# Mirrored score blocks in a symmetric attention, and a first stage ordered by what it needs, in a fused two-layer kernel on one core

## What is computed

```python
# layer 0, on g = groupnorm(x): attention over positions and a squeeze gate
q, k, v = Wq @ g + bq, Wk @ g + bk, Wv @ g + bv
out = v @ softmax(q.T @ k, axis=-1).T
y = sigmoid(relu(mean(g) @ se_w1.T) @ se_w2.T)
x = x + gamma * out + g * y
# layer 1, on tokens t = (batch, 2304, 128)
s = layernorm(t);  t = t + softmax(s @ s.T, axis=-1) @ s
u = layernorm(t);  t = t + top-2-of-8 experts(u)     # router softmax, gates renormalised
```

## Time and profile before

| | |
|---|---|
| time, median of 3 runs (lowest to highest) | 2839.08 us (2837.59 to 2839.95) |
| the profiled execution's own time | 2836.02 us |
| its span | 2834.2 us |
| TensorE busy | 2636.5 us, 93% |
| VectorE busy | 2161.3 us, 76% |
| ScalarE busy | 2023.1 us, 71% |
| GpSimd busy | 446.9 us, 16% |
| mean DMA rate | 8 GB/s |
| chain that ended last, by engine | PE 61%, DVE 23%, ACT 9%, issue 5%, POOL 2% |

### The profile page before, as it was taken

How to read it: one execution, slowest core, us unless ns; L and a number is a source line. 1 busy time by engine, 2 the same in 40 slices (tenths; PEclk the granted TensorE clock), 3 DMA queues, 4 the chain that set the end, 5 groups by cost and what they waited for, 6 DMA issues and landing times.

```text
span 2834.2 us, 45738 instructions
## 1 busy us (share of the span) xinstructions
PE 2636.5 (93%) x15334; PEld 2381.2 (84%) x15334; DVE 2161.3 (76%) x5499; ACT 2023.1 (71%) x4305; POOL 446.9 (16%) x840
## 2 busy tenths in 40 slices
PE   5999989999899998999989999999999999999996
PEld 4888978889788897889978898888988889888895
DVE  4886778787787877877778777887777877788775
ACT  2777767677676876768767687676867768677774
POOL 0000210032100331003200133001220022200223
PEclk7999999999999999999999999999999999999997
DMA  1000000000000000000000000000000000000000
GB/s 35 1 1 18 7 6 1 18 7 6 7 1 18 7 6 7 1 18 7 9 4 1 18 7 11 2 1 18 10 9 1 1 21 6 9 1 1 4 9 12
DMA packets 10037, 23.05 MB, mean 8 GB/s; under 512 B 1992, under 2 KB 8528, under 8 KB 8784
## 3 DMA queue, kind: packets, MB, share of 16 engines
q1 hardware_dynamic: 9808, 20.14, 2.0%
HBM read 10.70 MB, written 9.44 MB: 7 GB/s over the span
## 4 chain that ended last, share of the span: by engine, by line
PE 61%; DVE 23%; ACT 9%; issue 5%; POOL 2%; SPq 0%; DMA 0%; ACTq 0%; DVEq 0%; POOLq 0%
PE ps L1005 17%; PE ps L1007 17%; PE ps L1006 17%; PE ps L1018 9%; DVE mx L818 6%; DVE pt_lo L828 3%; DVE pt_lo L902 3%; ACT pt_hi L612 2%; ACT p_rows L600 2%; DVE u_tok L879 1%; ACT p_rows L647 1%; POOL u_rs L518 1%; ACT pt_hi L656 1%; ACT p_rows L681 1%; DVE acc L984 1%
## 5 line engine op out<-in xcount | busy, mean ns | idle before, releaser
L612 ACT ACTIVATE pt_hi<-ps 128x384 fp32r<-128x384 f32 x864 | 425.4, 492 | 319.2 <-PE ps L1018 313.5
L828 DVE TENSOR_TENSOR pt_lo<-ps,pt_hi 128x384 fp32r<-128x384 f32 x864 | 479.5, 556 | 178.7 <-ACT pt_hi L612 170.3
L600 ACT ACTIVATE p_rows<-ps,negmax 128x512 f32<-128x512 f32 (+1 forms) x720 | 464.8, 647 | 72.9 <-DVE negmax L822 65.8
L902 DVE TENSOR_TENSOR pt_lo<-p_rows,pt_hi 128x768 fp32r<-128x768 f32 x432 | 413.9, 959 | 124.1 <-ACT pt_hi L656 122.4
L818 DVE TENSOR_REDUCE mx<-ps 128x1 f32<-128x512 f32 (+1 forms) x720 | 442.0, 633 | 79.4 <-PE ps L1007 55.4
L1018 PE MATMUL ps<-ident,p_rows 128*128 128x128 f32 x2736 | 455.7, 275 | 40.4 <-DVE pt_lo L828 22.9
L647 ACT ACTIVATE p_rows<-ps,shift 128x768 f32<-128x768 f32 x432 | 389.6, 902 | 119.1 <-PE ps L1007 114.0
L1018 PEld LDWEIGHTS ps<-ident,p_rows 128*128 128x128 f32 x2736 | 332.4, 140 | 153.8 <-issue 54.9
L656 ACT ACTIVATE pt_hi<-p_rows 128x768 fp32r<-128x768 f32 x432 | 365.6, 846 | 40.1 <-PE ps L1007 0.7
L1005 PE MATMUL ps<-pt_hi,v_hi 128*128 128x384 f32 x864 | 358.6, 415 | 2.5 <-ACT y_out L621 2.5
L1005 PE MATMUL ps<-xt_hi 128*128 128x384 f32 x864 | 305.2, 353 | 0.0
(11 more groups left out here) (165 smaller groups left out, 5162.4 us busy)
## 6 DMA issues: line engine op xcount, KB each, us to landing
x_chan<-x SPq DMA_DIRECT2D x8, 1152.0 KB, 5.1
...
w_sb<-w SPq DMA_DIRECT2D x2, 4.0 KB
```

Source lines behind the costliest of these rows:

```text
L600: act.activation(p_rows[:, ROW_BUFFER[r, n % 2], a:a + w], ps[:, c, 0:w], ACT.Exp, bias=negmax[:, r % 2:r % 2 + 1], accum_out=dparts[:, n, ...
L612: act.activation(pt_hi[:, slot, :], ring_bank(step)[:, 0:BW], ACT.Copy)\
L828: dve.tensor_tensor(pt_lo[:, slot, :], ring_bank(step)[:, 0:BW], pt_hi[:, slot, :], ALU.subtract).then_inc(pt_lo_ready, 1)
L902: dve.tensor_tensor(p1_lo[:, w % 3, :], p1_f[:, w % 2, :], p1_hi[:, w % 3, :], ALU.subtract).then_inc(p1_lo_ready, 1)
```

## The change

It has two parts.

**Mirrored blocks.** A block (ib, j) with ib >= 1 whose key tile j lies in the query columns of ib-1 is the transpose of parts of six earlier blocks: of (ib-1, t) for the six tiles t in the columns of ib. That makes 6 blocks for ib = 1 (w = 18 to 23) and 6 for ib = 2 (w = 42 to 47), 12 of 54. The exponentials of the source blocks (`kept`, w = 6 to 11 and 30 to 35) stay in `p1_kept` (row buffers 1 and 2). For a mirrored block TensorE makes six transposes instead of six matmuls, ScalarE has one copy from PSUM instead of exponential and copy, and VectorE's `p1low` reads the PSUM banks. TensorE's block w+2 therefore waits for `p1low` of a mirrored w.

Row buffers 1 and 2 are now taken: the expert terms move to row buffer 4, and `xg_f` shrinks to one slot beside them. `xgnorm` waits for the low part of the one before; its slots go from 14, 15, 16 to 14, 16, 17.

**First stage.** The inputs are packed into 8 transfers, in the order of use, x in three thirds with a semaphore each (for all batches). The statistics wait only for their third. Keys and the first query come right after the variance; the squeeze gate, the values, the base, and the folding and splitting of the expert weights are spread over the 18 slots of the n = 0 rows. ScalarE makes some of the high parts that VectorE made.

```diff
+def mirrored(w):
+    ib, j = divmod(w, NT)
+    return ib >= 1 and (ib - 1) * LW <= j * TILE < ib * LW
+def kept(w):
+    ib, j = divmod(w, NT)
+    return ib + 1 < LB and (ib + 1) * LW <= j * TILE < (ib + 2) * LW
...
-NORMALISE_SLOTS = [14, 15, 16]
+NORMALISE_SLOTS = [14, 16, 17]
...
-def first_stage(b):
-    s = statistics(b) + normalise(b)
-    s += [(step[0], b, step[1]) for slot in sorted(PROJECT_SLOTS) for step in PROJECT_SLOTS[slot]]
-    return s + [step for j in range(NT) for step in attention0(b, 0, j)]
+def first_stage():
+    s = statistics(0)[:9]
+    s += [("xgnorm", 0, 0), ("xg", 0, 0), ("xgnorm", 0, 1), ("kproj", 0, 0), ("xg", 0, 1), ("kproj", 0, 1), ("xgnorm", 0, 2),
+          ("kproj", 0, 2), ("xg", 0, 2), ("qproj", 0, 0), ("kproj", 0, 3), ("kproj", 0, 4), ("kproj", 0, 5)]
+    rest = {1: [("gn_norm", 0)], 2: [("se_in", 0)], 3: [("se_out", 0)], 5: [("fold", 0, 0)], 7: [("fold", 0, 1), ("base", 0, 0)],
+            9: [("fold", 0, 2)], 11: [("foldsplit", 0)], 13: [("base", 0, 1)], 15: [("base", 0, 2)]}
+    merge(rest, {slot: [("vproj", 0, m)] for m, slot in enumerate([0, 2, 4, 8, 12, 16])})
+    merge(rest, {j: attention0(0, 0, j) for j in range(NT)})
+    return s + [step for j in range(NT) for step in rest[j]]
...
-        terms = p_rows[:, 2, 0:2 * 5 * 128].rearrange("p (s a w) -> p s a w", s=2, a=5)
+        terms = p_rows[:, 4, LW:LW + 2 * 5 * 128].rearrange("p (s a w) -> p s a w", s=2, a=5)
+        p1_kept = p_rows[:, 1:3, :].rearrange("p a w -> p (a w)").rearrange("p (s w) -> p s w", s=LW // TILE)
-        xg_f = p_rows[:, 4, :].rearrange("p (s w) -> p s w", s=LB)
+        xg_f = p_rows[:, 4, 0:LW]
...
+            load(0, 0)
+            sp.dma_start(w_stage[:, :, :], wqkv).then_inc(qkv_loaded, 16)
+            load(0, 1)
+            load(0, 2)
+            sp.dma_start(biases[:, 0:4], channel).then_inc(biases_loaded, 16)
+            sp.dma_start(se_sb[:, :], se).then_inc(se_loaded, 16)
+            sp.dma_start(fold_b, eb).then_inc(fold_loaded, 16)
+            sp.dma_start(fold_w, ew).then_inc(fold_loaded, 16)
...
+                elif kind == "mirror":
+                    act.wait_ge(s1_done, at(s1_done, *step))
+                    act.wait_ge(pv1_done, at(pv1_done, "pv1", b, w - 3))
+                    act.activation(thirds(p1_hi[:, w % 3, :]), p1_banks(w), ACT.Copy).then_inc(p1_hi_ready, 1)
...
+                    if u:
+                        dve.wait_ge(xg_lo_ready, at(xg_lo_ready, "xg", b, u - 1))
+                    elif b:
+                        dve.wait_ge(xg_lo_ready, at(xg_lo_ready, "xg", b - 1, LB - 1))
...
+                    if mirrored(w):
+                        dve.tensor_tensor(thirds(p1_lo[:, w % 3, :]), p1_banks(w), thirds(p1_hi[:, w % 3, :]),
+                                          ALU.subtract).then_inc(p1_lo_ready, 1)
...
+            def wait_s1_banks(b, w):
+                if mirrored(w - 2):
+                    pe.wait_ge(p1_lo_ready, at(p1_lo_ready, "p1low", b, w - 2))
+                else:
+                    pe.wait_ge(p1_exp_ready, at(p1_exp_ready, "s1", b, w - 2))
...
+                elif kind == "mirror":
+                    wait_s1_banks(b, w)
+                    pe.wait_ge(p1_exp_ready, at(p1_exp_ready, "s1", b, (ib - 1) * NT + (ib + 1) * LW // TILE - 1))
+                    for t in range(LW // TILE):
+                        ins = pe.transpose(ps[:, 2 * (w % 2) + t // TPB, t % TPB * 128:(t % TPB + 1) * 128],
+                                           p1_kept[:, t, j % (LW // TILE) * 128:(j % (LW // TILE) + 1) * 128], ident[:, :])
+                    ins.then_inc(s1_done, 1)
```

More of the change, by code:

```diff
@@ L161, in batch @@
         if w < end:
-            s.append(("s1", b, w))
+            s.append(("mirror" if mirrored(w) else "s1", b, w))
         if w == end + LAG - 1:
@@ L176, in batch @@
     return s
-PLAN = first_stage(0) + [step for b in range(B) for step in batch(b)]
+PLAN = first_stage() + [step for b in range(B) for step in batch(b)]
 RAISES = {
@@ L183 @@
     "se_in": ["ring_full", "se_hidden_ready"], "se_out": ["ring_full", "se_exp_ready"],
+    "fold": ["ring_full", "bias_left"], "foldsplit": ["bias_folded", "e_hi_ready", "e_split"],
     "xgnorm": ["xg_norm_ready"], "xg": ["xg_hi_ready", "xg_lo_ready"], "base": ["base_done"],
@@ L198 @@
 }
-LAST = {"gn_dev": "gn_dev_ready", "gn_var": "gn_var_ready", "se_in": "se_hidden_ready", "se_out": "se_exp_ready",
+LAST = {"fold": "bias_left", "gn_dev": "gn_dev_ready", "gn_var": "gn_var_ready", "se_in": "se_hidden_ready", "se_out": "se_exp_ready",
         "kproj": "k_lo_ready", "vproj": "v_lo_ready", "baset": "base_tok_ready",
@@ L419, in chained, with s1_kind, p1_rows, p1_banks @@
             return LINKS[step] + links
+        def s1_kind(w):
+            return "mirror" if mirrored(w) else "s1"
+        def p1_rows(w):
+            if kept(w):
+                return p1_kept[:, w % NT % (LW // TILE), :]
+            return p1_f[:, w % 2, :]
+        def p1_banks(w):
+            return ps[:, 2 * (w % 2):2 * (w % 2) + 2, 0:BW]
+        def thirds(ap):
+            return ap.rearrange("p (s w) -> p s w", s=2)
         def residual(m, k):
@@ L459, in _ @@
                     sp.wait_ge(ring_full, filled(("baset", b, NB - 1)))
-                    sp.dma_start(x_chan[:, :], x[b + 1]).then_inc(x_loaded, 16)
+                    for u in range(LB):
+                        load(b + 1, u)
                 if b:
@@ L538, in take @@
                         act.wait_ge(ring_full, filled(("qproj", b - 1, NB - 1)))
-                    act.activation(xg_hi[:, u * LW:(u + 1) * LW], xg_f[:, u, :], ACT.Copy)\
+                    act.activation(xg_hi[:, u * LW:(u + 1) * LW], xg_f, ACT.Copy)\
                         .then_inc(xg_hi_ready, 1)
@@ L562, in take @@
                     act.wait_ge(ring_full, filled(step))
+                    if m == 0 and not b:
+                        act.wait_ge(e_split, 2)
                     if m == 0 and b:
@@ L768, in take @@
                     dve.wait_ge(se_exp_ready, at(se_exp_ready, *step))
+                    if not b:
+                        dve.wait_ge(w_lo_ready, 2)
                     link(dve.tensor_scalar(se_tmp, se_e, 1.0, None, ALU.add))
@@ L997, in _ @@
             pe.wait_ge(consts_made, 12)
-            pe.wait_ge(w_loaded, 16 * N_WLOADS)
-            for i, (a, z) in enumerate(FOLD_PARTS):
-                pe.matmul(ps[:, i, 0:z - a], ones[:, :], fold_w[:, a:z], start=True, stop=True).then_inc(column_sums, 1)
-            pe.wait_ge(w_split, W_SPLITS)
             def three(out, lhs_hi, lhs_lo, rhs_hi, rhs_lo, start=True, stop=True):
@@ L1036, in take @@
                         .then_inc(ring_full, 1)
+                elif kind == "fold":
+                    a, z = FOLD_PARTS[step[2]]
+                    pe.wait_ge(fold_loaded, 32)
+                    wait_ring(step)
+                    pe.matmul(ring_bank(step)[:, 0:z - a], ones[:, :], fold_w[:, a:z], start=True, stop=True)\
+                        .then_inc(ring_full, 1)
                 elif kind == "se_in":
                     wait_ring(step)
+                    if not b:
+                        pe.wait_ge(se_loaded, 16)
                     pe.wait_ge(se_in_ready, at(se_in_ready, "gn_norm", b))
@@ L1054, in take @@
                     pe.wait_ge(xg_lo_ready, at(xg_lo_ready, "xg", b, m // 2))
+                    if not b and not m:
+                        pe.wait_ge(w_lo_ready, 1)
                     wait_ring(step)
@@ L1153, in take @@
                     m = step[2]
+                    if not b and not m:
+                        pe.wait_ge(e_split, 2)
                     pe.wait_ge(u_lo_ready, at(u_lo_ready, "ut", b, m))
```

150 lines of the change are left out of this document (77 added, 73 removed).

## The result

The changed kernel takes 2819.08 us (median of 4 runs, 2816.27 to 2820.85) against 2838.41 us (4 runs, 2837.59 to 2839.95) for the kernel before, measured beside it: ratio 0.993, 95% interval 0.9913 to 0.9948, 19.3 us less. Predicted were 2820. The profiled execution took 2820.85 us for a span of 2819.1.

A forecast was written before the change was run, and what follows sets the result against it. TensorE was taken to bound the kernel, VectorE and ScalarE close behind in blocks 18 to 23. The start's -17 and the second attention's -2 made -19 us, a median of 2820; range 2792 to 2836 for 8 in 10.

The forecast's parts named there:

- the start: First stage of batch 0: first scores 28 us earlier, 11 given back, so 17 us saved (13 to 21).
- the second attention: All eight batches' mirrored blocks: 7 x (2.2 - 1.8) - 4.8 = -2 us.
- Mirrored blocks on TensorE: Six transposes take 0.65 us against 1.04 for six matmuls, saving 0.4 us a block.
- Rival B: Transposes on TensorE are paced by their 275 ns: +58 us, less 17, giving 2880; chance 0.03.
- Reading PSUM: VectorE's low part of a mirrored block: 959 ns to 1.10 us, taken as 0.96.
- ScalarE's copy: In a mirrored block, the copy out of PSUM takes 799 ns against 846 from SBUF.
- The walk of the first six: Blocks 18 to 23: waits for xgnorm and low parts delay block 24, costing 2.2 us a batch.
- The second six: Blocks 42 to 47: block 45 waits for p1low(43), the rest run at TensorE's pace, saving 1.8 us a batch.
- Batch 7: The last batch has no projections, so neither stall: 12 x 0.4 = 4.8 us saved.
- Rival A: TensorE's saving in the mirrored blocks arrives whole, stalls falling into VectorE slack: 2784 us; chance 0.13.
- Rival C: Mirrored blocks' late low part grows into a second chain, the second six gaining nothing: +16, 2855 us; chance 0.07.
- given back: In the row phase after the first scores, moved first-stage work costs 11 us of the gain (7 to 15).

The follow-up runs named there:

- e4_nomirror_xg3: The changed kernel with no block mirrored and three slots for xg_f, so the new first stage alone: 2818.73 us.
- e1_xg3: The changed kernel with three slots for xg_f instead of one and xgnorm back at slots 14, 15, 16: 2793.53 us.
- e9_qsoon: e1_xg3 with the next batch's query projection put behind the low part of its block (43) on ScalarE and VectorE: 2808.12 us.
- e12_best: e11_soon2 with the query projection ahead of the low part of block 43 again: 2782.96 us.
- e11_soon2: e1_xg3 with the next batch's key, value and query projections all behind the low part of their block on ScalarE and VectorE: 2783.22 us.
- e6_base: e1_xg3 with the three residual-base passes moved out of the first three rows of batch 0 to behind them: 2795.23 us.

## Why the prediction was right

**The whole.** 2820 against 2819.08, faster, inside the range. In the traces the start brought 16.4 (17 predicted) and the second attention cost 1.8 where a gain of 2 was predicted; outside these two the traces differ by less than 1 us. Predicted were 19 us between the two traces, and they differ by 15.1. The medians differ by 19.3, since the profiled execution of the changed kernel was the slowest of its four. That a miss of 4 us in the second attention and 4 us between trace and median cancel is luck.

**Mirrored blocks on TensorE: right.** 0.4 us a block was predicted. Taking for each kind of row the median distance to the next start, blocks 18 to 24 hold 17.16 us of TensorE's work in e4_nomirror_xg3 and 14.80 in e1_xg3: 0.39 a block. Rival B is out. The groups of the changed kernel, in the columns of the earlier trace rows:

```profile
L957 DVE TENSOR_TENSOR pt_lo<-ps,pt_hi 128x768 fp32r<-128x768 f32 x96 | 89.7, 948 | 0.3 <-ACT pt_hi L703 0.3
L1204 PE MATMUL ps<-ident,p_rows 128*128 128x128 f32 x576 | 80.3, 276 | 3.1 <-DVE pt_lo L957 3.1
L703 ACT ACTIVATE pt_hi<-ps 128x768 fp32r<-128x768 f32 x96 | 78.3, 817 | 43.3 <-PE ps L1204 42.2
```

A transpose lasts 276 ns, and the next one starts 0.1 us after its start. The Trainium skill's 275 ns ("TensorE: Matmul & The Clock Gate", Part 4) agrees with this trace as a duration; the distance of starts is about a third of it. Reading PSUM costs VectorE nothing against SBUF: 948 ns, where the prediction allowed 959 to 1100; ScalarE's copy took 817 ns, not 799.

**The walk of the first six: right, in the order of waits and in time.** Batch 3 now runs 12.57 us earlier; with that taken off, the walk had block 20 at 1298.0, 21 at 1301.8, 23 at 1306.3 and 24 at 1310.0, and measured are 1298.21, 1301.83, 1306.48 and 1310.07. ScalarE's idle time was 3.18 for "about 3", the loss 2.0 to 2.6 us in batches 1 to 6 for 2.2. Batch 0 lost 1.8.

**The second six: the time nearly right, the wait not.** The prediction had block 45 wait for its bank pair, until p1low(43) is done. In batch 3 of the changed kernel (TensorE, then VectorE) it is the expert matmuls ahead of block 45 that wait, and for q_lo:

```profile
1374.86 0.50 PE L1059 MATMUL ps<-ew_hi,u_hi 128*128 128x512 f32 x1 [0.91 <-DVE q_lo L861]
...
1375.73 0.88 PE L1204 MATMUL ps<-ident,p_rows 128*128 128x128 f32 x6
```
```profile
1374.19 0.61 DVE L861 SCALAR_TENSOR_TENSOR q_lo<-ps,biases,q_hi 128x384 fp32r<-128x384 f32 x1
1374.72 0.95 DVE L957 TENSOR_TENSOR pt_lo<-ps,pt_hi 128x768 fp32r<-128x768 f32 x1
```

p1low(43) ends at 1375.67, just ahead of block 45, which waits for nothing. With the 10.24 us by which block 42 is earlier, block 45 stands at 1385.97, predicted 1385.9: the low part is done 0.06 us before the block, so the wrong wait gave the right start, which is luck. e9_qsoon and e12_best show which one binds. The six save 1.50 us a batch, not 1.8, since blocks 45 to 47 save 1.10 where the walk had 1.35, and blocks 48 to 53 give back 0.2, which the prediction didn't have. Batch 7 saves 5.5 for 4.8. These make nearly all of the 4 us by which the second attention missed.

**What the net hid.** The prediction netted saving and stall inside the first six blocks, which gives the right time and says little about the change. Taken apart, the mirrors are worth 25 us (with three slots) and the single slot costs 26. Rival A (2784, the saving arrives whole) failed for this kernel for the reason given, the order of VectorE's queue. With three slots and the projections behind the low parts the kernel takes 2783.2 us, but that closeness to 2784 doesn't prove rival A's sum: from e4_nomirror_xg3 to e11_soon2 blocks 18 to 24 fall by 21.6 us, and TensorE's saving there is 19. The rest comes with the new place of the projections. Rival C's bank wait is small: TensorE waited 3.1 us in all ahead of transposes for low parts (the group of L1204 above).

**The start: right in sum, terms off.** The last statistic ended at 9.6, not 7.5; the first scores came 26.2 us earlier, not 28; 9.9 were given back, not 11. These three are one execution's: under the same first stage the first scores came at 26.1 to 28.6 us and block 0 at 209.8 to 216.9, a gain of 12 to 20 us, so a closeness of 0.6 us to the predicted 17 is in part luck. What is given back isn't ScalarE's base passes (e6_base). In the changed kernel TensorE's projections run at the lower level up to the first scores: 384 columns start 0.32 us apart, though the clock column reads 1.00 (window and two rows of TensorE's timeline), where for most of the kernel before's value projections, at the lower level too, it reads 0.56 in the earlier trace rows:

```profile
12.80:28.50 15.70, 10.20 (x31) 8.03 (x31) 8.97 (x13) 6.15 (x10) 0.01 (x1) 1.00 0.00 0
```
```profile
24.58 0.52 PE L1061 MATMUL ps<-xg_hi,w_lo 128*128 128x384 f32 x1
24.90 0.61 PE L1059 MATMUL ps<-xg_hi,w_hi 128*128 128x384 f32 x1
```
